# Two sequences per output projection, in three products of rounded parts, turned back by a transpose

## The chip, the cores and the metric

The kernel runs on one core of a Trainium2 chip. The metric is the device time of one execution in microseconds, lower is better. A profile of one execution comes with it: its span runs from the first to the last instruction, and all times inside it count from the start of the span.

## What is computed

A decoder layer over 16 sequences of 128 tokens with 128 features, all in float32. The part that matters here is the multi-head attention that is run twice, first on the layer's own tokens ("sa"), then against a context ("ca"), with 16 heads of 64 features:

```
def attention(x, ctx, mask, wq, wk, wv, wo, bo):
    q, k, v = (x @ wq), (ctx @ wk), (ctx @ wv)          # split into 16 heads of 64
    sim = jnp.einsum('bhid,bhjd->bhij', q, k) * SCALE
    sim = jnp.where(mask[:, None, None, :], neg, sim)
    attn = jax.nn.softmax(sim, axis=-1)
    out = jnp.einsum('bhij,bhjd->bhid', attn, v).transpose(0, 2, 1, 3).reshape(b, n, 1024)
    return out @ wo + bo                                # the output projection
...
a = attention(x, x, ...);   x = layernorm(x + a, ln1_g, ln1_b)
a = attention(x, ctx, ...); x = layernorm(x + a, ln2_g, ln2_b)
h = gelu(x @ fc1_w + fc1_b); x = layernorm(x + h @ fc2_w + fc2_b, ln3_g, ln3_b)
```

Ahead of it stands a convolution mixer with a layer norm, and behind it a small mixture of experts with a last layer norm.

## The kernel before, in words

All engines run orders written out by hand; every dependence is a semaphore wait in the code. The work of both attentions is one list of 32 items (`ITEMS`): item n is sequence n % 16 of attention n // 16. A loop over p from 0 to 31 (VectorE: 1 to 32) handles several stages of neighbouring items at once. I call one turn of it "loop p". In loop p TensorE does, in this order (lines 736 to 757):

- `x_transpose(p-4)`, the transpose of the item's normalised result into the layout that the next product needs;
- `v_half(p, 0)` and `(p, 1)`, the values, three products of 512 columns each;
- `unit(p, 0..3)`, queries and keys for a later pair of sequences, six products of 256 columns each. Units 0 and 2 write PSUM bank 0 and are copied out by ScalarE (`q_out`), units 1 and 3 write bank 1 and are copied out by VectorE (`k_out`);
- `transposes(p-1, 0..3)`, four probability tiles each, into banks 2 and 3 in turn, copied out by VectorE (`pt_out`, line 1107);
- in loops 0 to 9 products of the mixer (`projection`, `mixer_output`, `x1_transposes`);
- `out_proj(p-2)`, the output projection of one item: eight float32 products of 128 columns (line 582);
- `scores(p+1)` (line 551), into banks 0 to 3, and `p_v(p-1)` (line 566), into banks 4 and 5, copied out by ScalarE (`ot_out`, line 844).

The queries, keys and values are made in "three products of rounded parts" (`mm_split`, line 70): each operand is held as a rounded high part (type fp32r) and a low part (the rest, also fp32r), and high times high, high times low and low times high are summed in PSUM.

`scores(p+1)` must wait for both `k_out` of loop p, since it overwrites bank 1, and in its second half for all four `pt_out`, since it overwrites banks 2 and 3. VectorE then takes 16 tiles of scores with `maxima` (line 1081), ScalarE makes the exponentials (`exps`, line 817), VectorE the reciprocals of the sums, and GpSimd multiplies (`normalise(p, g)`, line 1530). After the output projection VectorE does `residual` (sum, statistics), GpSimd a power (`inverse_deviation`), VectorE `normalise`, GpSimd `affine` and `next_residual`, TensorE `x_transpose`, ScalarE `xT_high` and VectorE `xT_low`. The projection and `x_transpose` share bank 7 (`W_BANK`), so they wait for one another's readers.

After the loops comes a tail, also by hand: the hidden layer (`hidden`, `fc2_sum`, line 289) for four groups of four sequences, between the last projections, then the layer norms and the experts. Its order on VectorE opens with

```
residual(ITEMS - 1); xT_low(ITEMS - 2); normalise(ITEMS - 1); residual_sum(0)
residual_moments(0); xT_low(ITEMS - 1); gained(0); outer_sums(0)
```

where `residual_sum(g)` is line 1265 and `gained(g)` line 1279.

## Time and profile before

| | |
|---|---|
| median of 3 runs | 501.43 us (501.26 to 502.74) |
| the profiled execution's own time | 501.12 us |
| its span | 499.2 us |
| TensorE matmul busy | 470.6 us, 94% |
| VectorE busy | 385.0 us, 77% |
| ScalarE busy | 366.8 us, 73% |
| GpSimd busy | 251.9 us, 50% |
| mean granted TensorE clock | 0.99 of full speed |

The profiled execution took 1.9 us more than its span. PE stands for TensorE, DVE for VectorE, ACT for ScalarE, POOL for GpSimd. A share of the whole span is an average over stages that have different limits; busy times in a stretch say more. A matmul's duration holds a latency that overlaps the next matmul, so what a matmul costs is read from the distance of two starts.

### The profile page before, as it was taken

The numbers are of one execution on the slowest core, as the hardware profiler recorded it, in microseconds if no ns is written. First come the engines' busy times: TensorE is split into PE (matmuls) and PEld (weight loads), VectorE is DVE, ScalarE is ACT, GpSimd is POOL, SyncE is SP. The second block draws the span as 40 slices with busy tenths as digits, with TensorE's granted clock in tenths as the row PEclk, the third lists the DMA queues.
The fourth block names the chain that finished last, engine by engine and source line by source line (L and its number), as shares of the span: only waits on it lengthen the run. The fifth ranks groups of instructions, "written<-read, shape, count | busy, mean of one in ns | idle before, by whom it ended". The sixth has DMA issues, their size and how long they took to land.

```text
span 499.2 us, 14097 instructions
## 1 busy us (share of the span) xinstructions
PE 470.6 (94%) x4644; PEld 431.5 (86%) x4644; DVE 385.0 (77%) x1852; ACT 366.8 (73%) x1390; POOL 251.9 (50%) x342
## 2 busy tenths in 40 slices
PE   4788999999999999999999999999999999999894
PEld 4678889999999999999999999999999997798672
DVE  4768778898888877887787777777777777538866
ACT  3547887868677788877778887777777777836763
POOL 1545357675565654555545454444554455633432
PEclk9999999999999999999999999999999999999987
DMA  8740000000000004000000000000000000400003
GB/s 242 233 195 2 1 3 1 2 2 2 1 3 1 2 2 126 1 4 1 3 1 2 2 2 1 3 1 3 3 1 3 1 2 3 169 1 0 7 13 90
DMA packets 15720, 14.18 MB, mean 28 GB/s; under 512 B 2848, under 2 KB 13344, under 8 KB 15520
## 3 DMA queue, kind: packets, MB, share of 16 engines
q1 hardware_dynamic: 14080, 12.81, 8.2%
q8 instruction: 38, 0.62, 0.5%
q10 hardware_dynamic: 1568, 0.47, 0.5%
q14 instruction: 34, 0.28, 0.2%
HBM read 12.10 MB, written 1.18 MB: 27 GB/s over the span
## 4 chain that ended last, share of the span: by engine, by line
PE 73%; DVE 13%; ACT 5%; issue 3%; DMA 2%; POOL 2%; SPq 1%; POOLq 0%; DVEq 0%; ACTq 0%
PE late_bank L582 10%; PE late_bank L534 10%; PE late_bank L551 10%; PE late_bank L566 10%; PE late_bank L72 8%; PE late_bank L74 8%; PE late_bank L73 8%; ACT P L817 3%; DVE P L1081 3%; DMA x<-in_xT 2%; PE late_bank L591 1%; DVE G L1198 1%; DVE ffstats L1253 1%; PE late_bank L608 1%; PE late_bank L610 1%
## 5 line engine op out<-in xcount | busy, mean ns | idle before, releaser
L817 ACT ACTIVATE P<-P,at_negmax 128x128 f32<-128x128 f32 x512 | 198.9, 396 | 79.1 <-DVE at_negmax L1081 79.1
L1530 POOL TENSOR_TENSOR P<-P,at_inv 128x512 f32<-128x512 f32 x128 | 136.6, 1078 | 123.2 <-DVE at_inv L1091 123.1
L1107 DVE COPY at_PT<-late_bank 128x512 f32<-128x512 f32 x128 | 87.7, 688 | 35.1 <-PE late_bank L534 34.9
L1081 DVE CUSTOM_DVE_ANT_0 P<-late_bank,maskb 128x128 f32<-128x128 f32 x512 | 110.5, 286 | 2.7 <-PE late_bank L551 2.7
L817 ACT ACTIVATION_READ_ACCUMULATOR P<-P,at_negmax 128x1 f32 x512 | 100.1, 195 | 0.0
L534 PE MATMUL late_bank<-ident,P 128*128 128x128 f32 x512 | 76.4, 273 | 2.0 <-DVE at_negmax L1081 1.0
L534 PEld LDWEIGHTS late_bank<-ident,P 128*128 128x128 f32 x512 | 59.8, 140 | 8.5 <-issue 4.0
L551 PE MATMUL late_bank<-at_k,at_q 64*128 64x128 f32 x1024 | 65.8, 278 | 0.9 <-DVE at_k L1099 0.9
L551 PEld LDWEIGHTS late_bank<-at_k,at_q 64*128 64x128 f32 x1024 | 59.7, 188 | 4.8 <-issue 1.2
L566 PE MATMUL late_bank<-at_PT,V 128*64 128x128 f32 x1024 | 63.0, 276 | 0.0
L566 PEld LDWEIGHTS late_bank<-at_PT,V 128*64 128x64 f32 x1024 | 55.2, 137 | 3.9
L1099 DVE COPY at_k<-late_bank 128x512 f32<-128x512 f32 x64 | 44.2, 691 | 8.1 <-PE late_bank L74 7.0
L1081 DVE DVE_READ_ACCUMULATOR2_ANT at_negmax<- 128x1 f32 x512 | 42.7, 83 | 0.0
L827 ACT ACTIVATE at_q<-late_bank 128x512 f32<-128x512 f32 x64 | 37.7, 589 | 4.0 <-PE late_bank L74 4.0
L1548 POOL TENSOR_TENSOR at_N<-at_N,row_ln_g 128x128 f32<-128x128 f32 x32 | 14.7, 460 | 49.8 <-DVE at_N L1132 49.8
L836 ACT ACTIVATE V<-late_bank 128x512 f32<-128x512 f32 x64 | 37.6, 587 | 0.0
L844 ACT ACTIVATE at_OT<-late_bank 128x512 f32<-128x512 f32 x64 | 34.3, 587 | 2.9 <-PE late_bank L566 2.9
L608 PE MATMUL late_bank<-xT_hi,w_hi 128*128 128x256 f32 x72 | 22.8, 317 | 11.2 <-DVE xT_lo L1155 7.1
L582 PE MATMUL late_bank<-wo_sa,at_OT 128*128 128x128 f32 x256 | 31.3, 276 | 0.6 <-DVE x1T_lo L1234 0.6
L582 PE MATMUL late_bank<-wo_ca,at_OT 128*128 128x128 f32 x256 | 31.2, 275 | 0.0
L582 PEld LDWEIGHTS late_bank<-wo_sa,at_OT 128*128 128x128 f32 x256 | 29.9, 192 | 1.0 <-issue 1.0
L582 PEld LDWEIGHTS late_bank<-wo_ca,at_OT 128*128 128x128 f32 x256 | 29.9, 192 | 0.1
(195 smaller groups left out, 1055.4 us busy)
## 6 DMA issues: line engine op xcount, KB each, us to landing
ctxT_raw<-in_ctxT SPq DMA_DIRECT2D x1, 1024.0 KB, 8.8
out<-xres SPq DMA_DIRECT2D x4, 224.0 KB, 2.6
x<-in_xT SPq DMA_DIRECT2D x1, 768.0 KB, 9.5
xres<-in_x SPq DMA_DIRECT2D x1, 768.0 KB, 14.0
tap_rows<-in_short_wT SPq DMA_DIRECT2D x3, 192.0 KB, 4.9
sa_wq_raw<-in_sa_wq SPq DMA_DIRECT2D x1, 512.0 KB, 7.4
sa_wk_raw<-in_sa_wk SPq DMA_DIRECT2D x1, 512.0 KB, 8.5
sa_wv_raw<-in_sa_wv SPq DMA_DIRECT2D x1, 512.0 KB, 9.8
```

The costliest lines, as they stand in the source:

```text
L72: nc.tensor.matmul(out, w.hi[wsel], x.hi[xsel], start=first, stop=False)
L73: nc.tensor.matmul(out, w.hi[wsel], x.lo[xsel], start=False, stop=False)
L74: return nc.tensor.matmul(out, w.lo[wsel], x.hi[xsel], start=False, stop=True)
L534: last = nc.tensor.transpose(banks[T_BANK[g % 2]][:, h * 128:(h + 1) * 128], P[:, n % 2, HQ * g + h, :], k.ident[:])
L551: last = nc.tensor.matmul(score_bank(h), q[rows, t % 2, h // 2, pair], kk[rows, t % 2, h // 2, pair], start=True, stop=True)
L566: last = nc.tensor.matmul(banks[O_BANK[h // 8]][part:part + 64, h // 2 % 4 * 128:(h // 2 % 4 + 1) * 128], V[:, n % 2, h * DH:(h + 1) * DH] ...
L582: last = nc.tensor.matmul(banks[W_BANK][:, 0:128], OT[:, n % 2, c, :], out_w[att(n)][:, c, :], start=(c == 0), stop=(c == H // 2 - 1))
L817: last = nc.scalar.activation(P[:, n % 2, h, :], P[:, n % 2, h, :], ACT.Exp, scale=-1.0, bias=negmax[:, n % 2, h:h + 1], accum_out=total[: ...
L1081: last = nc.vector.tensor_tensor_reduce(P[:, n % 2, h, :], score_bank(h), k.maskb[:, cols(n)], scale=1.0, scalar=3.0e38, op0=ALU.add, op1= ...
L1099: nc.vector.tensor_copy(kk[:, t % 2, u - 1:u + 1, :], banks[UNIT_BANK[1]][:].rearrange("p (h l) -> p h l", h=2)).then_inc(k_ok, 1)
L1107: nc.vector.tensor_copy(PT[:, HQ * g:HQ * g + HQ, :], banks[T_BANK[g % 2]][:].rearrange("p (h l) -> p h l", h=HQ)).then_inc(pt_ok, 1)
L1530: nc.gpsimd.tensor_tensor(tile, tile, inv[:, n % 2, HQ * g:HQ * g + HQ].unsqueeze(2).to_broadcast([128, HQ, 128]), ALU.mult).then_inc(norm ...
```

## The change

The output projection takes a pair of items at once and is split. Its operands become high and low parts: `ot_out` (ScalarE) writes the high part, the new `ot_low` (VectorE) the low part, once per half item; ScalarE and GpSimd make the parts of the weights once for each attention. The product is made the other way round, with the weights stationary and the 256 columns of a pair moving, so it comes out transposed; ScalarE copies it out (`out_turned`) and two TensorE transposes turn it back (`turn_back`). Residual, statistics, normalisation, affine, `x_transpose`, `xT_high` and `xT_low` are done per pair. The projection is cut into two halves: the first stands ahead of `scores` in odd loops, the second behind `v_half(p, 0)` in even loops. Buffers that the parts need are found by overlaying others; so the context is loaded only after the mixer's last gate, and the second attention's output weights after loop 13. The low parts of the second attention's weights are made two loops later (loops 4, 6, 8 for 2, 4, 6).

```diff
+        FIRST_HALF, SECOND_HALF, NORM = -3, -4, -5
+        def item_pair(p, lag):
+            t = (p + lag) // 2
+            return t if (p + lag) % 2 == 0 and 0 <= t < PAIRS else None
...
+            sp.wait_ge(c_mm, 3 * NPAIR)
+            sp.wait_ge(y_ok, NPAIR)
             sp.dma_start(k.raw["ctxT"][:], io["ctxT"]).then_inc(ld_w["ctxT"], 16)
...
+            def out_proj(t, half):
+                pe.wait_ge(ot_lo, 4 * t + 3 + half)
+                if half == 0:
+                    wait(pe, xT_lo, t)
+                    wait(pe, r_ok, t)
+                    wait(pe, x1lo, before(t + 4))
+                    pe.wait_ge(wo_lo, att_pair(t) + 1)
+                w = out_w[att_pair(t)]
+                for c in range(4 * half, 4 * half + 4):
+                    for wo, ot in ((w.hi, OT.hi), (w.hi, OT.lo), (w.lo, OT.hi)):
+                        last = nc.tensor.matmul(banks[W_BANK][:, 0:PCOLS], wo[:, c, :], ot[:, c, :], ...)
+            def turn_back(t):
+                pe.wait_ge(outT_ok, t + 1)
+                for b in range(PAIR):
+                    last = nc.tensor.transpose(turned_back()[:, b], outT[:, b * 128:(b + 1) * 128], k.ident[:])
...
             for p in range(ITEMS):                                   # TensorE
-                x_transpose(p - 4)
                 v_half(p, 0)
+                out_proj(item_pair(p, SECOND_HALF), 1)
                 unit(p, 0)
                 transposes(p - 1, 0)
                 unit(p, 1)
+                turn_back(item_pair(p, SECOND_HALF))
                 v_half(p, 1)
                 transposes(p - 1, 1)
                 unit(p, 2)
                 x1_transposes(p, transposed_in(p))
+                x_transpose(item_pair(p, NORM))
...
-                out_proj(p - 2)
+                out_proj(item_pair(p, FIRST_HALF), 0)
                 scores(p + 1)
                 p_v(p - 1)
-            x_transpose(ITEMS - 4)
+            out_proj(PAIRS - 2, 1)
             transposes(ITEMS - 1, 0)
             transposes(ITEMS - 1, 1)
...
             hidden(k, pe, 0, (0, 1))
             second_bias(0)
+            turn_back(PAIRS - 2)
             transposes(ITEMS - 1, 2)
             transposes(ITEMS - 1, 3)
-            out_proj(ITEMS - 2)
             p_v(ITEMS - 1)
-            x_transpose(ITEMS - 3)
             hidden(k, pe, 0, (2, 3))
-            out_proj(ITEMS - 1)
             wait_result(1)
             hidden(k, pe, 1, (0, 1))
-            x_transpose(ITEMS - 2)
+            x_transpose(PAIRS - 2)
+            out_proj(PAIRS - 1, 0)
+            out_proj(PAIRS - 1, 1)
             fc2_sum(k, pe, 0)
-            x_transpose(ITEMS - 1)
+            turn_back(PAIRS - 1)
             hidden(k, pe, 1, (2, 3))
             wait_result(2)
             hidden(k, pe, 2, (0, 1))
             next_fc2(1)
+            x_transpose(PAIRS - 1)
             hidden(k, pe, 2, (2, 3))
...
-                xT_high(p - 4)                                       # ScalarE
                 v_out(p, 0)
+                ot_out(p - 2, 0)
+                out_turned(item_pair(p, SECOND_HALF))
                 q_out(p, 0)
+                ot_out(p - 2, 1)
                 mixer_normal(transposed_in(p))
-                ot_out(p - 2, 0)
-                ot_out(p - 2, 1)
                 exps(p, 2)
                 x1_high(transposed_in(p))
+                xT_high(item_pair(p, NORM))
...
+            def ot_low(n, o):                                        # VectorE
+                vec.wait_ge(ot_ok, 2 * n + o + 1)
+                part = np.s_[:, 4 * o:4 * o + 4, n % 2 * 128:(n % 2 + 1) * 128]
+                nc.vector.tensor_tensor(OT.lo[part], banks[O_BANK[o]][:].rearrange("p (c l) -> p c l", c=4),
+                                        f32(OT.hi[part]), ALU.subtract).then_inc(ot_lo, 1)
...
-                normalise(p - 3)
+                normalise(item_pair(p, NORM))
                 reciprocals(p, 0)
                 reciprocals(p, 1)
-                xT_low(p - 4)
                 pt_out(p - 1, 0)
+                ot_low(p - 2, 0)
                 k_out(p, 1)
+                ot_low(p - 2, 1)
+                residual(item_pair(p, SECOND_HALF))
                 pt_out(p - 1, 1)
+                statistics(item_pair(p, SECOND_HALF))
                 pt_out(p - 1, 2)
                 x1_low(transposed_in(p))
+                xT_low(item_pair(p, NORM))
                 k_out(p, 3)
                 pt_out(p - 1, 3)
...
-                if p in (2, 4, 6):
-                    weight_low(CA[p // 2 - 1])
+                if p in (4, 6, 8):
+                    weight_low(CA[p // 2 - 2])
...
-                residual(p - 2)
                 reciprocals(p, 3)
                 maxima(p + 1, 0)
                 maxima(p + 1, 1)
-            normalise(ITEMS - 2)
-            xT_low(ITEMS - 3)
-            residual(ITEMS - 1)
-            xT_low(ITEMS - 2)
-            normalise(ITEMS - 1)
+            ot_low(ITEMS - 1, 0)
+            ot_low(ITEMS - 1, 1)
+            normalise(PAIRS - 2)
+            xT_low(PAIRS - 2)
+            residual(PAIRS - 1)
+            statistics(PAIRS - 1)
             residual_sum(0)
+            normalise(PAIRS - 1)
             residual_moments(0)
-            xT_low(ITEMS - 1)
+            xT_low(PAIRS - 1)
             gained(0)
```

## Rows read from the trace of the kernel before

**Rows 1.** Windows: two loops of the mixer's stage, one later loop, the tail's two parts.
```profile
core 0: us, PE busy (x) PEld busy (x) DVE busy (x) ACT busy (x) POOL busy (x), PEclk, DMA share, GB/s
102.96:116.86 13.90, 13.82 (x143) 12.80 (x142) 11.49 (x57) 11.18 (x44) 8.95 (x11) 1.00 0.01 2
116.86:131.13 14.27, 14.27 (x149) 13.54 (x149) 12.23 (x57) 10.95 (x44) 8.35 (x12) 1.00 0.01 3
...
302.53:314.48 11.95, 11.95 (x129) 11.21 (x129) 9.41 (x48) 9.32 (x39) 5.96 (x9) 1.00 0.01 2
...
431.39:449.38 17.99, 17.99 (x169) 16.57 (x170) 7.07 (x24) 8.09 (x14) 7.43 (x16) 1.00 0.01 2
449.38:482.98 33.60, 30.78 (x192) 24.84 (x190) 28.21 (x142) 22.77 (x47) 13.19 (x13) 0.95 0.02 4
```

**Rows 2.** Timeline of TensorE through one later loop: start, us, what.
```profile
302.46 2.06 PE L551 MATMUL late_bank<-at_k,at_q 64*128 64x128 f32 x32
...
304.44 1.97 PE L566 MATMUL late_bank<-at_PT,V 128*64 128x128 f32 x32
...
306.34 0.33 PE L591 MATMUL late_bank<-ident,at_X 128*128 128x128 f32 x1
...
306.43 0.48 PE L72 MATMUL late_bank<-ca_wv_hi,ctxT_hi 128*128 128x512 f32 x1
...
307.21 0.28 PE L72 MATMUL late_bank<-x1T_hi,ca_wq_hi 128*128 128x256 f32 x1
...
307.93 0.60 PE L534 MATMUL late_bank<-ident,P 128*128 128x128 f32 x4
...
308.28 0.37 PE L72 MATMUL late_bank<-ctxT_hi,ca_wk_hi 128*128 128x256 f32 x1
...
309.08 0.40 PE L72 MATMUL late_bank<-ca_wv_hi,ctxT_hi 128*128 128x512 f32 x1
...
312.10 0.60 PE L534 MATMUL late_bank<-ident,P 128*128 128x128 f32 x4
...
312.53 1.95 PE L582 MATMUL late_bank<-wo_ca,at_OT 128*128 128x128 f32 x16
...
314.41 2.06 PE L551 MATMUL late_bank<-at_k,at_q 64*128 64x128 f32 x32
```

**Rows 3.** Timeline of VectorE in the same loop: the first maximum, and what follows the last.
```profile
303.67 0.29 DVE L1081 CUSTOM_DVE_ANT_0 P<-late_bank,maskb 128x128 f32<-128x128 f32 x1
...
307.05 0.34 DVE L1132 TENSOR_SCALAR at_N<-at_R,at_mv,at_rstd 128x128 f32<-128x128 f32 x1
```

**Rows 4.** Timeline of VectorE: two copies back to back; a mixer residual with its statistics.
```profile
434.66 1.28 DVE L1107 COPY at_PT<-late_bank 128x512 f32<-128x512 f32 x2
...
115.43 0.41 DVE L1207 TENSOR_TENSOR R<-late_bank,xres 128x256 f32<-128x256 f32 x1
...
116.76 0.17 DVE L1091 RECIPROCAL at_inv<-at_total 128x4 f32<-128x4 f32 x1
```

**Rows 5.** Groups by form: operations like those added or merged, mean ns of one.
```profile
L1265 DVE TENSOR_TENSOR ffR<-late_bank,xres 128x512 f32<-128x512 f32 x4 | 2.8, 690 | 2.2 <-PE late_bank L289 2.2
...
L844 ACT ACTIVATE at_OT<-late_bank 128x512 f32<-128x512 f32 x64 | 34.3, 587 | 2.9 <-PE late_bank L566 2.9
...
L1601 POOL TENSOR_TENSOR x<-N,row_ln_b 128x256 f32<-128x256 f32 x8 | 5.9, 733 | 0.0
```

**Rows 6.** Timeline of VectorE in loop 6: the last `pt_out`, then `weight_low` after the convolution.
```profile
128.49 0.68 DVE L1107 COPY at_PT<-late_bank 128x512 f32<-128x512 f32 x1
...
131.06 1.20 DVE L1239 TENSOR_TENSOR ca_wv_lo<-ca_wv_raw,ca_wv_hi 128x1024 fp32r<-128x1024 f32 x1
```

**Rows 7.** The tail: `fc2_sum(0)` in the chain of waits, VectorE's `residual_sum(0)` and `gained(0)`.
```profile
445.76 3.59 PE late_bank L289 x32
...
449.38 0.69 DVE L1265 TENSOR_TENSOR ffR<-late_bank,xres 128x512 f32<-128x512 f32 x1 [2.25 <-PE late_bank L289]
...
451.70 1.13 DVE L1279 SCALAR_TENSOR_TENSOR N<-ffR,ffmv,ln_g 128x128 f32<-128x128 f32 x4
```

**Rows 8.** DMA issues of the page: the load of the context, KB, us to landing.
```profile
ctxT_raw<-in_ctxT SPq DMA_DIRECT2D x1, 1024.0 KB, 8.8
```

More of the change, by code:

```diff
@@ L503, in unit @@
                     if a:
-                        wait(pe, xT_lo, 2 * t + 2 - NSEQ)
+                        wait(pe, xT_lo, t + 1 - NPAIR)
                     else:
@@ L584, in out_proj @@
                 last.then_inc(o_mm, 1)
-            def x_transpose(n):
-                if not exists(n):
+            def turn_back(t):
+                if t is None:
                     return
-                wait(pe, x_ok, n + 1)
-                wait(pe, r_ok, min(n + 2, ITEMS))
-                nc.tensor.transpose(banks[W_BANK][:, 0:128], X[:], k.ident[:]).then_inc(xT_mm, 1)
+                pe.wait_ge(outT_ok, t + 1)
+                for b in range(PAIR):
+                    last = nc.tensor.transpose(turned_back()[:, b], outT[:, b * 128:(b + 1) * 128], k.ident[:])
+                last.then_inc(back_mm, 1)
@@ L593, in projection, with x_transpose @@
+            def x_transpose(t):
+                if t is None:
+                    return
+                wait(pe, x_ok, t + 1)
+                wait(pe, x1lo, before(t + 5))
+                for b in range(PAIR):
+                    last = nc.tensor.transpose(banks[W_BANK][:, b * 128:(b + 1) * 128], X[:, b], k.ident[:])
+                last.then_inc(xT_mm, 1)
             def projection(p, m, c):
@@ L1127, in normalise @@
-            def normalise(n):
-                if not exists(n):
-                    return
-                vec.wait_ge(rstd_ok, n + 1)
-                wait(vec, x_ok, n)
-                nc.vector.tensor_scalar(N[:], R[:], mv[:, 0:1], rstd[:, 0:1], ALU.subtract, ALU.mult).then_inc(n_ok, 1)
-            def xT_low(n):
-                if not exists(n):
-                    return
-                vec.wait_ge(xT_hi, n + 1)
-                out = results[att(n)]
-                nc.vector.tensor_tensor(out.lo[:, cols(n)], banks[W_BANK][:, 0:128], f32(out.hi[:, cols(n)]),
+                vec.wait_ge(ot_ok, 2 * n + o + 1)
@@ new lines, in statistics @@
+            def statistics(t):
+                if t is None:
+                    return
+                vec.wait_ge(r_ok, t + 1)
+                for b in range(PAIR):
+                    last = nc.vector.bn_stats(stats[:, b], R[:, b])
+                last.then_inc(st_ok, 1)
+                vec.wait_ge(st_ok, 2 * t + 1)
+                for b in range(PAIR):
+                    last = nc.vector.bn_aggr(mv[:, b], stats[:, b])
+                last.then_inc(st_ok, 1)
+                vec.wait_ge(st_ok, 2 * t + 2)
+                nc.vector.tensor_scalar(mv[:, :, 1], mv[:, :, 1], EPS, None, ALU.add).then_inc(mv_ok, 1)
@@ new lines, in normalise, with xT_low @@
+            def normalise(t):
+                if t is None:
+                    return
+                vec.wait_ge(rstd_ok, t + 1)
+                wait(vec, x_ok, t)
+                for b in range(PAIR):
+                    last = nc.vector.tensor_scalar(N[:, b], R[:, b], mv[:, b, 0:1], rstd[:, b:b + 1], ALU.subtract,
+                                                   ALU.mult)
+                last.then_inc(n_ok, 1)
+            def xT_low(t):
+                if t is None:
+                    return
+                vec.wait_ge(xT_hi, t + 1)
+                out = results[att_pair(t)]
+                nc.vector.tensor_tensor(out.lo[:, pcols_pair(t)], banks[W_BANK][:, 0:PCOLS], f32(out.hi[:, pcols_pair(t)]),
```

225 lines of the change are left out of this document (128 added, 97 removed).

## The prediction

> **What bounds the kernel now.** I read three views in this order. The windows by loop [rows 1] show who is full: in the later loops TensorE is busy 11.95 of 11.95 us and VectorE 9.41, in the mixer's loops TensorE 13.82 of 13.90 and 14.27 of 14.27, VectorE 11.49 and 12.23. So TensorE sets the pace, and VectorE has 15 to 20% left. The tail is two stretches: up to 449.38 TensorE is again full (17.99 of 17.99); after it VectorE is (28.21 of 33.60, its waits being for GpSimd's powers in a chain with it). The timeline of TensorE [rows 2] then gives the place of each step in a loop, and that of VectorE [rows 3] how near it runs behind.
>
> I count from the start of `v_half(p, 0)` (306.43). Before it lie `scores` 1.98, `p_v` 1.90, `x_transpose` 0.09. Behind it: `v_half` 0.78, a unit 0.72 (0.80 behind transposes, as switching back from float32 costs 0.08), four transposes 0.35, their results 0.60 after their start; transposes(p-1, 0) at 1.50, `out_proj` at 6.10, next `scores` at 7.98 [rows 2].
>
> **The change on TensorE.** Removed in each loop: a projection, 1.88 from 312.53 to 314.41, and an `x_transpose`, 0.09 [rows 2]. Added for a pair: 24 products of 256 columns at 0.12 (six take the 0.72 of a unit), 2.86 in all or 1.43 a half; two turning transposes, 0.18 plus 0.08 for the switch; two `x_transpose` at 0.09 beside other transposes, 0.2. So `scores` comes at 7.98 - 1.88 + 1.43 + 0.26 = 7.79 in even loops, at 7.98 - 1.88 + 1.43 + 0.2 = 7.73 in odd ones, and a pair of loops needs 0.63 less TensorE time than the 23.9 it takes now. Over 16 pairs this is 10 us: all that the change can bring.
>
> **The change on VectorE.** Each `ot_low` reads 512 columns from PSUM and is priced by `residual_sum`, 690 ns [rows 5]; back to back such operations follow at 0.60 [rows 4] (unshown in this form; bounds are 0.60 and 0.69, I take 0.60). Two a loop add 1.2. Merging gives back some 0.2 a loop: one sum, one epsilon and one `xT_low` for two items. VectorE goes to about 10.4 of 11.6. That would fit on average; its order decides.
>
> *Even loop, later stage.* The second half of the projection now stands ahead of transposes(p-1, 0), so these start at 1.50 + 1.43 = 2.93 and end at 3.53. VectorE has ended the maxima and reciprocals by 1.6 and waits. From 3.55 to `scores` it must do, in order, `pt_out`, `ot_low`, `k_out`, `ot_low`, `residual`, `pt_out`, `statistics`, `pt_out`, `k_out`. Seven operations of 512 columns: 6 at 0.60 and the last at its full 0.69, 4.29. Residual and statistics of a pair take 1.33 in the mixer [rows 4], 1.2 here as a `pt_out` lies between. End: 9.05, and `scores` can start at 9.1 instead of 7.79, since it overwrites the bank that `k_out` reads: **1.3 us of waiting that is new**. Today three such operations stand there and nothing else. What is late next: `maxima(p+1)` start 1.21 after `scores` [rows 2, 3] and ScalarE follows them, so all shift by as much and nothing is made up. *Odd loop:* transposes end at 2.1, six operations end before 6.0, `xT_low` and `k_out` by 7.0, ahead of `scores`. But the first half waits for `xT_low` (same bank): `x_transpose` at 4.5 waits for GpSimd's two operations of 0.733 [rows 5], which start at 1.4, so it is in time; `xT_high` comes after `exps(p, 2)`, `xT_low` ends about 6.4 where 6.3 was wanted: 0.1. Sum for a later pair: -0.63 + 1.3 + 0.1 = +0.8.
>
> *Mixer's loops.* In even loops two projections stand between the transposes and `scores`, at 10.1, and the nine operations fit. But the convolution follows the last `pt_out`: that ends at 10.0, the convolution takes 1.97 (131.06 - 128.49 - 0.60), `weight_low` 1.20 [rows 6]. Maxima then start at 13.2 with `weight_low`, 1.9 late, end 3.38 later [rows 3], and the next loop's transposes, which overwrite score banks, wait 1.25 for them.
>
> *Other engines.* ScalarE gets a copy of 256 columns a pair and the weights' high parts; at 9.32 of 11.95 it stays hidden [rows 1]. GpSimd makes two low parts of weights in loops 2 and 17; with 5.96 to 8.95 busy per loop it hides them, and merged layer norms cost it nothing more. The context's load, 8.8 us [rows 8], moves behind loop 8's gate and is wanted at the end of loop 11, over 30 us later; if that cover went, ScalarE's rounding and the units of loop 15 would wait by as much as it is late. The second output weights load after loop 13 and are wanted in loop 19. All at nothing.
>
> **Stage by stage.** Loops 2 and 3: item 0's projection is gone from loop 2 (-1.9), loop 3 has a half instead of a whole (-0.45), and a `weight_low` went (-0.25): -2.6. Loops 4 to 7: two pairs at -0.63, two late `weight_low` at +1.0 beyond what is waited today: +0.7. Loops 8 to 11: loop 8 has convolution and `weight_low` with no projection to cover them: 1.4 ahead of `scores`, 1.9 more at the next transposes; loop 10 waits 1.4, of which some 0.9 are waited now; -1.3 of work: +2.5. Loops 12 to 29: nine pairs at 0.8, +7.2. Loops 30 and 31 have no units and follow the exponentials as now: 0.
>
> *The tail,* counted from the end of the last projection in a loop (431.39 now). Today: `fc2_sum(0)` ends at 18.0, `gained(0)` starts at 20.3 [rows 1, 7]. New on TensorE: `p_v` 1.9, the second half 1.5, transposes, two hidden chunks, bias, turn back at 6.3. VectorE waits for this with `residual` (6.5), and behind it stand `pt_out` 1, statistics, `pt_out` 2 and 3: end 9.65. `p_v` of the last item waits for that until 9.7 instead of 8.05, ends at 11.6. Its `ot_out` (0.59 each [rows 5]) and `ot_low` stand ahead of `normalise(14)`, 13.5; GpSimd's two operations: 15.15; `x_transpose(14)`, `xT_high`, `xT_low`: 16.45. Only then may the last pair's projection start in the same bank: 19.4, and `fc2_sum` (3.59) ends at 23.0, 5.0 later than now. Now VectorE: the last `residual` and statistics stand ahead of `residual_sum(0)`, and `xT_low(15)` ahead of `gained(0)`, while `x_transpose(15)` stands behind `fc2_sum(1)`: turn back 0.2, four hidden chunks 3.1, `fc2_sum(1)` 3.6, transpose, `xT_high` and `xT_low` 1.2: 31.1. **`gained(0)` starts 10.8 later than now**, and what follows is the chain VectorE bounds, so it shifts whole: +10.8.
>
> **Sum.** 501.12 (the profiled execution, 1.9 over its span, 0.3 under the median) - 2.6 + 0.7 + 2.5 + 7.2 + 10.8 = 519.7; I say 519.
>
> One rule speaks to the tail. The clock is at full speed in the full stretch before 449.38 and 0.95 of it after, where TensorE has gaps, so some time there ran at 1.2 GHz [rows 1]. In my schedule TensorE waits some 3.5 us for `residual_sum(1)` ahead of `fc2_sum(2)`; at 1.2 GHz that sum would take 3.6 more. The Trainium skill (TensorE: Matmul & The Clock Gate, "HAM oscillation") says that gaps between bursts re-throttle the array; the row agrees that the clock falls in this stage, and by the rule the time would be up to 523.
>
> **Rivals.**
> - *Loops stay TensorE's, the tail loses.* If VectorE's nine operations took 4.2 us instead of 5.5, no `scores` would wait; loops 4 to 31 would give about -9 and with -2.6 and the tail 500 to 506. For it: VectorE's average fits. Against it: 0.60 and 0.69 are rows, and nothing of the nine is optional.
> - *Faster.* The mechanism is the full 10 us of TensorE with the tail's work hidden. It needs the order on VectorE not to matter: `gained(0)` no more than about 8 us late with all loops bound by TensorE, 491 to 499. For it: the tail before 449.38 has VectorE busy only 7.07 of 17.99 [rows 1]. Against it: the queue is in order, and `xT_low(15)` waits behind `fc2_sum(1)` whatever VectorE's load.
> - *The clock falls in the tail, or even loops also hold back ScalarE*: 523 to 532. For it the clock's 0.95; against it, only one gap of mine is long.
> - *The change doesn't do what it says:* products are 24 a pair, by its own lines; not likely.
>
> **Numbers.** Forecast case 0.68 (510 to 524), TensorE-bound loops with a late tail 0.12, faster 0.08, slower still 0.12. The unknowns are `ot_low` (0.09 each, 60 times: 5 us), the fit of even loops (0.4 in eleven) and the tail's waits (half of 10.8). Cutting 5 off each side from these gives 507 to 529. A difference under 0.3%, 1.5 us, can't be told from none. Faster 0.10, same 0.04, slower 0.86.
>
> **What would show it.** Right: in even loops a wait of TensorE for `k_out` of 1 to 1.5 us ahead of `scores` and none in odd ones; loops of about 12.9 and 11.8; VectorE idle near 1.9 us before the first `pt_out` of even loops; `fc2_sum(0)` to `gained(0)` some 8 us apart for 2.3 now. Wrong: even loops below 12 us (VectorE's operations cheaper than priced), products of 256 columns further apart than 0.12, or the chain behind `gained(0)` having slack that takes up the delay.

## The result, and the profile after

The changed kernel takes 526.64 us (median of 4 runs, 524.42 to 527.35), the kernel before 501.35 (501.03 to 502.74) beside it: **1.049 times as long, 95% interval 1.046 to 1.052**. Forecast: 519, between 507 and 529. The profiled execution of after is its shortest, 524.42, span 522.5; that of before has a span of 499.2. The 23.3 between these two are what the views below place. Two executions (1116.51 us of the kernel before, beside e10 and e11, and 764.65 us of e12) were over half as long again as all others and are in no ratio.

The waits of TensorE in the profile after (line, what it waited for: us in total, times, longest us):

```profile
PE late_bank L588 <- DVE at_k L1171: 14.6, 12, 1.3
...
PE late_bank L298 <- DVE ffR L1357: 4.3, 2, 3.4
...
PE late_bank L603 <- DVE at_PT L1179: 1.4, 1, 1.4
```

The first line is new but for one of its waits: `scores` (L588) waits for `k_out` (L1171) in the eleven even loops from 8 to 28, 1.03 us in loops 8 and 10 and 1.3 us in each of the nine later ones, 13.7 in all. The twelfth, 0.88 us ahead of `scores(0)`, stands in the profile of before as well, and there it is the only one. The windows of after, by the same columns as [rows 1]: an even and an odd later loop, then the tail cut at the end of `fc2_sum(0)` and at the start of `gained(0)`:

```profile
297.40:310.49 13.09, 11.79 (x125) 10.98 (x125) 9.48 (x49) 9.87 (x41) 4.45 (x5) 1.00 0.01 2
310.49:322.44 11.95, 11.94 (x124) 11.00 (x124) 10.41 (x50) 9.51 (x39) 6.53 (x8) 1.00 0.01 2
...
444.10:467.40 23.30, 19.84 (x175) 17.24 (x175) 7.24 (x17) 8.56 (x14) 4.44 (x8) 1.00 0.01 2
467.40:475.38 7.98, 7.79 (x53) 6.79 (x52) 4.44 (x19) 3.19 (x6) 3.86 (x5) 1.00 0.00 1
475.38:508.00 32.62, 23.95 (x160) 19.18 (x158) 27.67 (x142) 22.06 (x47) 12.16 (x12) 1.00 0.03 5
```

The even loop is 1.3 longer than TensorE's busy time in it, and VectorE is busy for only 9.48 of its 13.09: the engine that TensorE waits for has room, but not at that place. The timeline of VectorE in this loop (start us, us) shows the queue that the prediction laid out against [rows 3]:

```profile
304.85 0.69 DVE L1179 COPY at_PT<-late_bank 128x512 f32<-128x512 f32 x1 [1.88 <-PE late_bank L571]
305.46 0.68 DVE L1188 TENSOR_TENSOR at_OT_lo<-late_bank,at_OT_hi 128x512 fp32r<-128x512 f32 x1
306.06 0.68 DVE L1171 COPY at_k<-late_bank 128x512 f32<-128x512 f32 x1
306.65 0.68 DVE L1188 TENSOR_TENSOR at_OT_lo<-late_bank,at_OT_hi 128x512 fp32r<-128x512 f32 x1
307.25 0.42 DVE L1200 TENSOR_TENSOR at_R<-late_bank,xres 128x256 f32<-128x256 f32 x1
307.58 0.68 DVE L1179 COPY at_PT<-late_bank 128x512 f32<-128x512 f32 x1
308.18 0.48 DVE L1207 BATCH_NORM_STATS2 at_stats<-at_R 128x6 f32<-128x128 f32 x2
308.69 0.25 DVE L1211 BATCH_NORM_AGGREGATE at_mv<-at_stats 128x2 f32<-128x6 f32 x2
308.98 0.17 DVE L1214 TENSOR_SCALAR at_mv<-at_mv 128x2 f32<-128x2 f32 x1
309.06 0.69 DVE L1179 COPY at_PT<-late_bank 128x512 f32<-128x512 f32 x1
309.66 0.68 DVE L1171 COPY at_k<-late_bank 128x512 f32<-128x512 f32 x1
```

It is idle for 1.88 until the first transposes (L571) come, behind the second half of the projection. From then on it never stops for 5.49 us (304.85 to 310.34); the last entry of these lines is the one that `scores` waits for. TensorE's own timeline closes the step:

```profile
301.28 0.50 PE L72 MATMUL late_bank<-ca_wv_hi,ctxT_hi 128*128 128x512 f32 x1
...
308.60 0.60 PE L571 MATMUL late_bank<-ident,P 128*128 128x128 f32 x4
310.49 0.71 PE L588 MATMUL late_bank<-at_k,at_q 64*128 64x128 f32 x8 [1.30 <-DVE at_k L1171]
```

`v_half` starts at 301.28, and the last transposes at 308.60 take 0.35 of issue, so `scores` could have started at 308.95, 7.67 behind `v_half`; it starts at 9.21. The 1.30 in brackets counts from the modelled end of the transposes, the full loss is 1.54.

The tail, on TensorE, answers to [rows 7]:

```profile
453.76 1.97 PE L603 MATMUL late_bank<-at_PT,V 128*64 128x128 f32 x32 [1.40 <-DVE at_PT L1179]
...
460.72 0.35 PE L621 MATMUL late_bank<-at_OT_hi,wo_ca_hi 128*128 128x256 f32 x1 [0.98 <-issue]
463.66 3.73 PE L298 MATMUL late_bank<-fc,P 128*128 128x128 f32 x32
...
470.64 3.73 PE L298 MATMUL late_bank<-fc,P 128*128 128x128 f32 x32
474.20 0.38 PE L641 MATMUL late_bank<-ident,at_X 128*128 128x128 f32 x2
...
481.16 3.84 PE L298 MATMUL late_bank<-fc,V 128*128 128x128 f32 x32 [3.38 <-DVE ffR L1357]
```

and on VectorE:

```profile
468.99 0.69 DVE L1357 TENSOR_TENSOR ffR<-late_bank,xres 128x512 f32<-128x512 f32 x1
...
475.04 0.42 DVE L1231 TENSOR_TENSOR x1T_lo<-late_bank,x1T_hi 128x256 fp32r<-128x256 f32 x1 [2.90 <-ACT x1T_hi L918]
475.38 1.13 DVE L1371 SCALAR_TENSOR_TENSOR N<-ffR,ffmv,ln_g 128x128 f32<-128x128 f32 x4
```

`gained(0)` (L1371) stands behind `xT_low(15)` (L1231), which waits 2.90 for a chain that begins with `x_transpose(15)` (L641) behind `fc2_sum(1)`: the averages that it reads had been ready since 471.7.

Where the 23.3 lie, by the starts of `scores` in both traces (it also has e7 and e10, told below):

| part | before, us | after | change | forecast | e7 | e10 |
|---|---|---|---|---|---|---|
| loops 2 and 3 | 28.83 | 26.73 | -2.1 | -2.6 | 26.73 | 26.70 |
| loops 4 to 7 | 56.34 | 57.83 | +1.5 | +0.7 | 56.51 | 56.50 |
| loops 8 to 11 | 49.93 | 52.71 | +2.8 | +2.5 | 50.39 | 50.38 |
| loops 12 to 29 | 215.16 | 225.52 | +10.4 | +7.2 | 219.96 | 214.66 |
| loop 30 to the end | 89.16 | 99.82 | +10.7 | +10.8 | 93.82 | 94.53 |
| an even / odd later loop | 11.95 / 11.95 | 13.09 / 11.96 | | 12.97 / 11.71 | 12.14 / 11.96 | 12.14 / 11.73 |

A loop here is counted from one `scores` to the next; up to loop 2 the two differ by 0.1.

### The profile page after: what moved, and what is told of

It is laid out like the page before. It is cut to its first block, busy times and chain, and to the rows that moved or that the text cites. A ratio compares the mean times of both kernels' runs of the same rounds, so it can differ in the third digit from the quotient of the medians.

```text
span 522.5 us, 13807 instructions
## 1 busy us (share of the span) xinstructions
PE 466.5 (89%) x4548; PEld 422.7 (81%) x4548; DVE 403.8 (77%) x1868; ACT 377.6 (72%) x1392; POOL 241.9 (46%) x280
## 4 chain that ended last, share of the span: by engine, by line
PE 57%; DVE 24%; issue 8%; ACT 3%; DMA 3%; POOL 2%; SPq 1%; POOLq 0%; DVEq 0%
PE late_bank L588 10%; PE late_bank L621 9%; PE late_bank L603 9%; PE late_bank L571 7%; PE late_bank L72 6%; PE late_bank L74 5%; PE late_bank L73 5%; DVE at_k L1171 4%; DVE P L1153 3%; DVE at_PT L1179 2%; DVE at_OT_lo L1188 2%; DMA x<-in_xT 2%; ACT P L871 2%; DVE G L1290 2%; PE late_bank L298 1%
## 5 line engine op out<-in xcount | busy, mean ns | idle before, releaser
L871 ACT ACTIVATION_READ_ACCUMULATOR P<-P,at_negmax 128x1 f32 x512 | 98.8, 193 | 0.0
L571 PE MATMUL late_bank<-ident,P 128*128 128x128 f32 x512 | 76.7, 273 | 5.5 <-DVE at_negmax L1153 3.5
L588 PE MATMUL late_bank<-at_k,at_q 64*128 64x128 f32 x1024 | 66.0, 278 | 15.0 <-DVE at_k L1171 14.6
L588 PEld LDWEIGHTS late_bank<-at_k,at_q 64*128 64x128 f32 x1024 | 60.1, 188 | 20.3 <-issue 17.4
L571 PEld LDWEIGHTS late_bank<-ident,P 128*128 128x128 f32 x512 | 59.8, 140 | 11.7 <-issue 6.6
L1640 POOL TENSOR_TENSOR at_rstd<-at_mv,half_neg 128x2 f32<-128x2 f32 x16 | 11.3, 706 | 82.7 <-DVE at_mv L1214 82.7
L1171 DVE COPY at_k<-late_bank 128x512 f32<-128x512 f32 x64 | 43.7, 683 | 6.4 <-PE late_bank L74 6.4
L881 ACT ACTIVATE at_q<-late_bank 128x512 f32<-128x512 f32 x64 | 37.9, 592 | 13.7 <-PE late_bank L74 13.7
L1188 DVE TENSOR_TENSOR at_OT_lo<-late_bank,at_OT_hi 128x512 fp32r<-128x512 f32 x64 | 43.5, 683 | 2.9 <-ACT at_OT_hi L898 2.6
L898 ACT ACTIVATE at_OT_hi<-late_bank 128x512 fp32r<-128x512 f32 x64 | 37.2, 584 | 3.6 <-PE late_bank L603 3.6
L1163 DVE RECIPROCAL at_inv<-at_total 128x4 f32<-128x4 f32 x128 | 20.5, 170 | 13.8 <-ACT P L871 12.5
L1651 POOL TENSOR_TENSOR at_N<-at_N,row_ln_g 128x256 f32<-128x256 f32 x16 | 11.8, 738 | 32.5 <-DVE at_N L1222 32.5
L659 PEld LDWEIGHTS late_bank<-xT_hi,w_hi 128*128 128x128 f32 x72 | 14.5, 201 | 12.3 <-issue 8.9
```

The lines of the kernel that those rows point to most:

```text
L571: last = nc.tensor.transpose(banks[T_BANK[g % 2]][:, h * 128:(h + 1) * 128], P[:, n % 2, HQ * g + h, :], k.ident[:])
L588: last = nc.tensor.matmul(score_bank(h), q[rows, t % 2, h // 2, pair], kk[rows, t % 2, h // 2, pair], start=True, stop=True)
L871: last = nc.scalar.activation(P[:, n % 2, h, :], P[:, n % 2, h, :], ACT.Exp, scale=-1.0, bias=negmax[:, n % 2, h:h + 1], accum_out=total[: ...
L881: nc.scalar.activation(q[:, t % 2, u:u + 2, :], banks[UNIT_BANK[0]][:].rearrange("p (h l) -> p h l", h=2), ACT.Copy, scale=NEG_SCALE).then ...
L1171: nc.vector.tensor_copy(kk[:, t % 2, u - 1:u + 1, :], banks[UNIT_BANK[1]][:].rearrange("p (h l) -> p h l", h=2)).then_inc(k_ok, 1)
L1188: nc.vector.tensor_tensor(OT.lo[part], banks[O_BANK[o]][:].rearrange("p (c l) -> p c l", c=4), f32(OT.hi[part]), ALU.subtract).then_inc(ot ...
```

## The experiments

**The theory** is that of the forecast case: two places in VectorE's order cost the time, the queue between the first transposes and `k_out(p, 3)` in even loops, and the last pair's place in the tail. **Rivals:** VectorE's added load as such (two `ot_low` a loop, 43.5 us in all), the place of the second half on TensorE, and the falling clock. Each of the kernels below is the changed kernel with one edit, from e7 on with several.

**e1: no low parts.** The calls of `ot_low` go, and the waits on them become waits on `ot_out`:

```diff
-                    for wo, ot in ((w.hi, OT.hi), (w.hi, OT.lo), (w.lo, OT.hi)):
+                    for j, wo in enumerate((w.hi, w.hi, w.lo)):   # all with OT.hi
...
-                ot_low(p - 2, 0)
-                ot_low(p - 2, 1)
```

> Leaves out the low part of the attention output: no ot_low on VectorE, and the second of the three products takes the high part again, so TensorE still makes all 24 products. If VectorE's queue between transposes(p-1, 0) and k_out(p, 3) is what holds scores in even loops, taking 1.2 us out of it takes 1.2 of the 1.3 us wait away: even loops go from 13.09 to about 11.9, the odd ones lose at most 0.2, the mixer's loops some, the tail about 1; median near 508 (from 526.6). If instead it is the turned product itself (its place ahead of the transposes, the shared bank 7, the turning back) that costs, the loops stay at 13.09 and 11.96 and the time within 2 us of 526.6.

Measured: 518.26 us, 1.034 times before (1.030 to 1.038). Even later loops take 12.44. Two operations of 0.60 went, but only 0.65 came back:

```profile
302.61 0.41 DVE L1200 TENSOR_TENSOR at_R<-late_bank,xres 128x256 f32<-128x256 f32 x1
303.36 0.69 DVE L1179 COPY at_PT<-late_bank 128x512 f32<-128x512 f32 x1 [0.33 <-PE late_bank L571]
```

The queue is now so early that its second `pt_out` waits 0.33 for the second transposes. So my 508 was wrong: I had taken the added time off the end of the queue and not looked at when each entry's input comes; the tail gained nothing either (91.5 us from the last `scores` to the end, after 89.6). As a verdict on load against order it says that without any load from the low parts TensorE still waits, 7.7 us in the eleven even loops.

**e2: statistics behind the last `pt_out`.** The same work in another place, in all loops:

```diff
-                statistics(item_pair(p, SECOND_HALF))
                 pt_out(p - 1, 2)
                 x1_low(transposed_in(p))
                 xT_low(item_pair(p, NORM))
                 k_out(p, 3)
                 pt_out(p - 1, 3)
+                statistics(item_pair(p, SECOND_HALF))
```

> The change, but statistics(t) stands behind pt_out(p-1, 3) on VectorE instead of ahead of pt_out(p-1, 2). Nothing waits for it before the next loop. By the queue theory the 0.88 us that it takes leaves the stretch ahead of k_out(p, 3): even loops from 13.09 to 12.2, wait for k_out from 1.3 to 0.4, eleven such loops: about -9 us, and 0.7 in the tail; median near 517. If VectorE's total work were the limit, moving an operation would change nothing: 526.

Measured: 523.22 us, 1.043 (1.036 to 1.050). Even later loops take 12.24, as the theory had it. But loops 5, 7 and 9 of the mixer went from 14.44, 14.40 and 13.93 to 15.33, 15.27 and 16.36, and loop 13 from 11.94 to 12.75: there the convolution or a low part stands behind the last `pt_out` and ahead of the next maxima, and the statistics came on top. The gain in one stage was paid back in the other, which I had not forecast.

**e3: another order in the tail.** On TensorE (VectorE and ScalarE follow, and VectorE takes `normalise(14)` ahead of the last `ot_low`):

```diff
+            turn_back(PAIRS - 2)
             hidden(k, pe, 0, (0, 1))
             second_bias(0)
-            turn_back(PAIRS - 2)
...
+            x_transpose(PAIRS - 2)
             wait_result(1)
             hidden(k, pe, 1, (0, 1))
-            x_transpose(PAIRS - 2)
             out_proj(PAIRS - 1, 0)
             out_proj(PAIRS - 1, 1)
-            fc2_sum(k, pe, 0)
-            turn_back(PAIRS - 1)
             hidden(k, pe, 1, (2, 3))
+            turn_back(PAIRS - 1)
+            fc2_sum(k, pe, 0)
+            x_transpose(PAIRS - 1)
             wait_result(2)
             hidden(k, pe, 2, (0, 1))
             next_fc2(1)
-            x_transpose(PAIRS - 1)
```

> The change with only the tail reordered: turn_back(14) ahead of the first hidden chunks, normalise(14) ahead of the last ot_low, x_transpose(14) one step earlier, hidden(1, (2, 3)) between the last pair's projection and its turn_back, that ahead of fc2_sum(0), and x_transpose(15) directly behind fc2_sum(0). By my schedule gained(0) starts about 6 us earlier (31.3 us after the last projection in a loop becomes about 25) and the chain behind it moves whole: median near 520. If the tail is bound by the amount of TensorE work, or the chain behind gained(0) has slack, less than 2 us come of it.

Measured: 519.01 us, 1.035 (1.031 to 1.040). The loops are those of after to 0.02; from the last `scores` to the end it is 81.8 us, where after has 89.6 and before 78.5. The timeline of VectorE shows why: no wait of 2.90 is left between the moments of group 0 and `gained(0)` (L1370), which now starts 24.9 behind the last projection in a loop, where after has 31.3.

```profile
467.41 0.69 DVE L1356 TENSOR_TENSOR ffR<-late_bank,xres 128x512 f32<-128x512 f32 x1 [0.71 <-PE late_bank L298]
...
469.54 0.42 DVE L1230 TENSOR_TENSOR x1T_lo<-late_bank,x1T_hi 128x256 fp32r<-128x256 f32 x1
469.87 1.13 DVE L1370 SCALAR_TENSOR_TENSOR N<-ffR,ffmv,ln_g 128x128 f32<-128x128 f32 x4
```

**e4: the last `k_out` by ScalarE**, in all loops but 0:

```diff
                 v_out(p, 1)                    # ScalarE
+                if p:
+                    k_out_late(p, 3)           # the same copy, by ScalarE
...
-                k_out(p, 3)                    # VectorE
                 pt_out(p - 1, 3)
```

> The change, but k_out(p, 3) of loops 1 to 29 is done by ScalarE behind v_out(p, 1), which takes 0.6 us off VectorE and puts 0.59 on ScalarE. By the queue theory k_out is then done about 8.15 us after v_half instead of 9.1: the wait ahead of scores goes from 1.3 to 0.4, even loops 12.2, about -10 us; median near 517. If ScalarE has no room (exps of the next loop late), the gain is under 3 us and ACT's wait for maxima, 68.5 us in all now, shrinks without gain.

Measured: 519.88 us, 1.036 (1.031 to 1.041). Even loops take 12.14, odd ones still 11.96; loops 13, 17 and 19 have 12.28, 12.87 and 12.86, of which more below, and loop 2 went from 13.19 to 14.19, which I had not forecast. VectorE's queue was what `scores` waited for; the 0.36 us that is left in each even loop is a wait for the same copy on ScalarE.

**e5: the second half behind the first transposes:**

```diff
-                out_proj(item_pair(p, SECOND_HALF), 1)
                 unit(p, 0)
                 transposes(p - 1, 0)
+                out_proj(item_pair(p, SECOND_HALF), 1)
```

> The second half of the projection stands behind unit(p, 0) and transposes(p-1, 0) instead of ahead of them; nothing is left out or reordered on VectorE. Theory (VectorE's queue between the first transposes and k_out(p, 3) is what TensorE waits for): VectorE gets its first pt_out 1.43 us earlier, but the two ot_low and the k_out of unit(p, 1) behind it then start earlier too, and residual still has to wait for the turned result, which comes no earlier than now; so only a part of the 1.43 comes through: even loops 12.7 for 13.09, 522 to 523 us in all. Rival (it is only the place of the half): the whole wait of 1.3 goes in each of the later even loops and 1 us in the mixer's even loops, 509 to 511 us.

Measured: 521.64 us, 1.040 (1.037 to 1.043); even loops 12.69, in the mixer 14.10 for 14.50. VectorE's timeline: its first `pt_out` is no longer late by 1.88, but the queue stops at its third entry.

```profile
300.71 0.69 DVE L1179 COPY at_PT<-late_bank 128x512 f32<-128x512 f32 x1 [0.43 <-PE late_bank L571]
301.32 0.68 DVE L1188 TENSOR_TENSOR at_OT_lo<-late_bank,at_OT_hi 128x512 fp32r<-128x512 f32 x1
302.88 0.69 DVE L1171 COPY at_k<-late_bank 128x512 f32<-128x512 f32 x1 [0.87 <-PE late_bank L74]
```

So the place of the half on TensorE is not the cause by itself: 0.40 a loop comes back, not 1.3, as said beforehand.

**e7: several places at once.** All the work is kept: the tail of e3; `k_out(p, 3)` by ScalarE in even loops from 4 on; the statistics behind the last `pt_out` from loop 12 on only; and

```diff
-                if p in (4, 6, 8):
+                if p in (5, 7, 9):
                     weight_low(CA[p // 2 - 2])
```

> All of the work is kept, its order is not: the tail's order of e3, k_out(p, 3) of the even loops from 4 on by ScalarE, the statistics behind the last pt_out from loop 12 on only, and weight_low in loops 5, 7 and 9 instead of 4, 6 and 8. Theory (a few queue places cost the time, and their costs add up): even later loops 12.1 for 13.09, odd ones 11.96, so loops 12 to 29 give back 8.5 us; the tail gives back 7.5; loops 4 to 11 give back about 2.5 (even loops lose the late weight_low, about 1 us each in three loops, odd loops get up to 0.3 each). 526.6 - 18.5 = about 507 us (505 to 510). Rival (the three gains cover one another, since all of them give VectorE's time): 513 us or more.

Measured: 509.34 us, 1.015 (1.012 to 1.018). The table has it by parts: loops 4 to 11 lose 3.6 of the 4.3 that they had cost. Loops 5, 7 and 9 give 0.67, 0.67 and 1.17 of this; the copy of k on ScalarE alone gave 0.16, 0.14 and 0.04 there (e4), so some 0.5, 0.5 and 1.1 are the place of `weight_low`. The other 1.1 is the copy's, in loops 8 and 10. The gains add up, except in loops 13, 17 and 19: 12.70, 12.88 and 13.45.

**e8 and e9.** e8 is e7 with one edit more, which gives TensorE something to do while ScalarE copies (the copy of these values goes behind `exps(p, 3)` on ScalarE). e9 is e8 with `xT_low` ahead of `pt_out(p-1, 2)` from loop 12 on and another order in the tail: `fc2_sum(0)` stands ahead of the last pair's projection, and that pair's `residual` and statistics stand behind `gained(0)` on VectorE.

```diff
                 transposes(p - 1, 3)
+                if p % 2 == 0 and p >= 12:
+                    v_half(p, 1)               # was ahead of transposes(p-1, 1)
```

> e7, and in even loops from 12 on v_half(p, 1) stands behind transposes(p-1, 3) and its copy behind exps(p, 3), so that TensorE has work while ScalarE makes k_out(p, 3). Theory: the last 0.34 us of TensorE's wait for k_out goes in each of nine even loops, even loops 11.8, 503 to 504 us. Rival (ScalarE's exponentials or VectorE's maxima set the pace below 12.1): even loops stay at 12.1, 507 us.

> e8, and from loop 12 on xT_low stands ahead of pt_out(p-1, 2), and in the tail fc2_sum(0) stands ahead of the projection of the last pair, whose residual and statistics come behind gained(0) and outer_sums(0) on VectorE, with GpSimd's two powers for group 0 ahead of those for the last pair. Theory: odd loops 11.80 for 11.96 (TensorE no longer waits 0.17 for xT_low ahead of the first half), 1.4 us in nine loops; gained(0) some 5 us earlier than in e8, of which 3 come through because the last pair's x_transpose and hidden(3) come later. 503.5 - 1.4 - 3 = 499 us (497 to 502), so no slower than the kernel before. Rival (the tail's end is set by the last pair's result and not by group 0): 502 us, the same as the kernel before.

Measured: e8 510.89 us, 1.017 (1.014 to 1.021), even loops 12.23 for 12.14. Nothing was gained, as the rival had it, but not for the rival's reason. From loop 12 on the wait for `k_out` is gone, and another of nearly its size stands ahead of the last transposes (L571), whose bank VectorE's second `pt_out` has to empty first:

```profile
304.92 0.63 PE L571 MATMUL late_bank<-ident,P 128*128 128x128 f32 x4 [0.32 <-issue]
```

VectorE ended that `pt_out` at about 304.8 (started as the first of two at 304.14). e9: 507.64 us, 1.015 (1.011 to 1.019). Its odd loops take 11.72, for 11.96: the 0.24 that TensorE had lost there came from `xT_low`'s place in VectorE's queue. The tail did not gain the 3 us forecast: from the last `scores` to the end the profiled executions have 86.7 us for e9 and 84.5 for e8, both at a mean clock of 0.982.

**e10: e9 with the large single operations moved too** (ScalarE's high part of the context also comes earlier), and e8's edit taken back:

```diff
-                elif p in (12, 13):
-                    context_low(p - 12)
-                elif p == NSEQ:
+                elif p in (11, 13):
+                    context_low(p // 2 - 5)
+                elif p == NSEQ + 1:
                     feed_forward_low()
-                elif p == NSEQ + 2:
+                elif p == NSEQ + 3:
                     bias_low()
```

> e9 with v_half(p, 1) back in its old place, and with the low parts of the context, of the feed-forward weights and of the biases made on VectorE in loops 11, 13, 17 and 19 instead of 12, 13, 16 and 18 (ScalarE's high part of the context one loop earlier where the load allows it). Theory (e8 only moved TensorE's wait from k_out(p, 3) to VectorE's pt_out ahead of the last transposes; and loops 13, 17 and 19 of e7 to e9 are late because a large extra operation on VectorE stood in the even loop ahead of them, which in the changed kernel the wait for k_out covered): even later loops 12.14 for 12.23, loops 13, 17 and 19 within 0.4 of the 11.72 of the other odd ones, 2 to 3 us less than e9: 504 to 506 us. Rival (VectorE is simply full, so the work comes up in another loop): 507.5 us, and loops 12 to 20 add up to as much as in e9.

Measured: 504.60 us (median of 12 runs), 1.0056 (1.0032 to 1.0081). Loops 13, 17 and 19 take 11.69, 11.73 and 11.73. VectorE was not full; these operations had stood in even loops, behind the last `pt_out` and ahead of the next maxima. In the changed kernel the 1.3 us for which `scores` waits in the same even loop had covered them: the first maximum of loops 13, 17 and 19 starts 1.65, 1.20 and 1.82 us behind its `scores` there, 2.47, 2.64 and 3.22 in e7, and 1.54 in e10. In loops 17 and 19 of e7 part of this is a wait of the low part for ScalarE's high part (0.60 and 0.99). This is the best of my versions, and it is still 0.6% slower than the kernel before.

**e11: products that fill two waits of the tail**, nothing else:

```diff
+            filler(13)                         # 128x512 products, result unread
             next_fc2(2)
...
+            filler(12)
             z_transposes(1)
```

> The changed kernel with 25 more products of 128x512 in the tail, whose result nobody reads (their bank is written anew later): 13 where TensorE waits 3.4 us ahead of fc2_sum(2) and 12 where it waits 3.2 us ahead of z_transposes(1), 3.05 and 2.8 us of work, so that they fit in the waits. Theory (the clock falls behind these waits in most executions, though not in the one profiled; that is why the median stands 2.2 us over the profiled execution): the mean clock is 0.99 or more in nearly all runs, and the median 524 to 525 us, below 526.6. Rival (the clock does not go by these waits, or its falls cost nothing): clocks from 0.98 on as before and 526 to 527 us, or more by the products' own time.

Measured: 526.19 us (522.84 to 526.97, 6 runs), 1.048 (1.045 to 1.051). The waits shrank from 3.38 to 0.38 and from 3.23 to 0.44, and the mean clocks are 0.989 to 0.997 where the four runs of after have 0.979 to 0.995. The median fell by 0.45, which is less than these runs scatter. My theory that the median would come down to 524 to 525 is not borne out. In e11's profiled execution the granted clock is 1.00 from 420 to 450 us, 0.83 in the window from 450 to 460, and 1.00 again up to 508: that fall comes ahead of both filled waits, so filling them could not prevent it.

**e12: e10 with the tail of e3, and ScalarE copies k ahead of v:**

```diff
-                v_out(p, 1)
                 if p % 2 == 0 and p > 2:
                     k_out_late(p, 3)
+                v_out(p, 1)                    # from loop 12 on, in even loops
```

> e10 with the tail of e3, and in even loops from 12 on ScalarE copies k_out(p, 3) ahead of v_out(p, 1) instead of behind it. Theory: the copy starts with the end of unit(p, 3) and not 0.2 us behind it, so TensorE's last wait of 0.36 shrinks to 0.15 to 0.2 and even loops take 11.95 to 12.0 for 12.14, 1.3 to 1.7 us in nine loops; the tail costs 3 us over that of the kernel before. 504.6 - 1.5, and the tail's end within 1 us of e10's: 502 to 503.5 us, 0.1 to 0.5% over the kernel before. Rival (v_out a little later holds back exps(p, 3) and with it the next transposes): even loops shorter and odd ones longer by as much, 504 to 505 us.

Measured: 506.03 us, 1.011 (1.007 to 1.015). Even loops stay at 12.14, odd ones go from 11.73 to 12.06: no gain, and the price that the rival had named in odd loops (0.33 each) with it. From the last `scores` to the end it has 82.2 us, e10 84.3 in its profiled execution, whose clock was 0.985 against 0.994.

## Why the prediction was right, step by step

**The mechanism was right**, and by the view that was to show it. `scores` waits 1.30 for `k_out` in even later loops (said: 1.3; between 1 and 1.5) and in none of the odd ones; VectorE stands idle 1.88 ahead of the first `pt_out` (said: near 1.9); its queue takes 5.49 (said: 5.5); `ot_low` follows at 0.60 like a copy. e2 and e4 take one entry out of this queue, by its place and by its engine, and give back 0.85 and 0.95 a loop. In the tail the last item's `p_v` starts 9.66 behind the last projection in a loop (said: 9.7), the last pair's projection 16.62 (said: 16.45), `fc2_sum(0)` ends 23.3 behind it (said: 23.0), and 8.0 pass from there to `gained(0)` (said: 8).

**The size was partly off.** The median of 526.64 lies above the forecast case's own 510 to 524 and 7.6 above the 519; it is inside the range of 507 to 529, and by its number alone it would fall to the case of 523 to 532. What the traces show is the mechanism of the forecast case with terms that were too small. The range does not quite follow from its own working either: its three unknowns (5, 4.4 and 5.4 us) add up to 14.8, and with 5 off that is 9.8 on each side of 519, 509 to 529.

**TensorE's saving was right in the later loops**, 0.63 a pair, though by two misses that cancel. Even loops: ready for `scores` at 7.67 (said: 7.79), with `scores` and `p_v` 11.55. Odd loops: 11.73 in e10, where nothing stands in their way (said: 7.73, with the same two 11.61). Together 23.28, the forecast's own sum, but the even loop is 0.12 shorter than said and the odd one 0.12 longer: that is luck. The 11.55 was never reached, though; 12.14 is what the best runs have (e10: `scores` starts 0.59 late, behind ScalarE's copy). e8 shows what stands behind one wait there, namely the next one in VectorE's queue.

**Mis-sized terms.**
- *Loops 12 to 29, +7.2 forecast, +10.4 measured.* A pair costs 1.14 and not 0.8, by three parts. The first is the step "`xT_low` ends about 6.4 where 6.3 was wanted: 0.1". VectorE took `xT_low` only behind the `pt_out` ahead of it, at 320.33; TensorE was ready for the first half at 320.59 (transposes 320.24, 0.35 of issue) and started it at 320.85. That is 0.26 (e9: 0.24), for I had placed `xT_low` by its input and not by its queue:

```profile
320.33 0.41 DVE L1231 TENSOR_TENSOR x1T_lo<-late_bank,x1T_hi 128x256 fp32r<-128x256 f32 x1
...
320.85 0.36 PE L621 MATMUL late_bank<-at_OT_hi,wo_ca_hi 128*128 128x256 f32 x1
```

  The second part, 0.12, is TensorE's work in odd loops, in which the switch from these products back to `scores` costs 0.08 (322.24 to 322.44, for a spacing of 0.12). The third, 0.11, stands in even loops: `scores` starts at 9.21, not 9.1, 0.15 behind the end of the copy.
- *Loops 4 to 7, +0.7 forecast, +1.5 measured.* The late `weight_low` was put at 1.0 a pair and is some 0.5 by e7 and e4. What failed is the other part, "-0.63" of TensorE's work a pair, with no wait beside it: with `weight_low` and the copy of k out of the way (e7) a pair takes 28.27 (14.50 and 13.77) against 28.18 before. In the even loops the wait that holds them is one that the forecast did not have. `x1_transposes` (L685) writes the same bank 7 in which the turned result lies until VectorE's `residual` (L1200) has read it:

```profile
125.96 0.41 PE L685 MATMUL late_bank<-ident,N 128*128 128x128 f32 x2 [0.24 <-DVE at_R L1200]
```

  The product ahead of it starts at 125.45 and takes 0.12 of issue, so 0.39 is lost (in loop 6 of e7 it is 0.26 ahead of `turn_back` and 0.08 here). In e5 and e1 `residual` is in time, this spacing is 0.12, and these loops take 14.10 and 14.07. In the odd loops of e7 the first transposes start 0.51 and 0.48 later than the products ahead of them would let them, waiting for the maxima; before, that was 0.24. These two come to 0.65 of the 0.72 that are missing.
- *Loops 8 to 11, +2.5 forecast, +2.8 measured.* This near hit is partly luck too. Loops 8 and 9 cost 2.1 where the forecast's terms give 1.4 + 1.9 - 0.63 = 2.7, and loops 10 and 11 cost 0.7 where they give 0.5 - 0.63 = -0.1. The wait of 0.39 for `residual` stands in loops 8 and 10 as well.
- *Loops 2 and 3, -2.6 forecast, -2.1 measured.* Loop 2 gave its 1.93; loop 3 gave 0.17 and not 0.7.
- *The tail, +10.8 forecast:* +11.0 up to `gained(0)`, 0.4 back behind it and 0.1 in loops 30 and 31.

**The sum** of the misses, 0.5 + 0.8 + 0.3 + 3.2 - 0.1 = 4.7, takes 519.7 to the 524.42 of the profiled execution. The median is 2.2 above that.

**The clock.** In the profiled execution the granted clock stayed at 1.00, the higher level, through the wait of 3.38 us and up to 508 us. In e5's trace, with the same tail and the same wait (474.7 to 478.12), it fell to 0.50, the lower level, while TensorE stood idle in it:

```profile
472.09:475.49 3.40, 2.46 (x10) 1.42 (x8) 3.33 (x13) 1.37 (x2) 0.00 (x0) 1.00 0.00 0
475.49:478.89 3.40, 0.77 (x3) 0.77 (x4) 2.25 (x13) 1.39 (x4) 1.99 (x2) 0.68 0.00 0
478.89:482.29 3.40, 3.40 (x18) 3.40 (x17) 3.12 (x17) 2.94 (x7) 1.11 (x1) 0.50 0.02 5
```

These are three windows by the columns of [rows 1]; TensorE was busy for 0.77 of the second, and 1.00 and 0.50 are its levels of 2.4 and 1.2 GHz. So the same schedule has its clock fall in one execution and not in another. The Trainium skill (TensorE: Matmul & The Clock Gate, "HAM oscillation") tells of a kernel in which the gap between two bursts re-throttled the array each time; e5's trace agrees, after's does not. What one fall costs can be read from the sum behind this wait, `fc2_sum(2)`:

```profile
478.12 6.40 PE L298 MATMUL late_bank<-fc,V 128*128 128x128 f32 x32 [3.38 <-DVE ffR L1357]
484.36 0.60 PE L699 MATMUL late_bank<-ident,N 128*128 128x128 f32 x4
```

From its start to the next transposes are 6.24 us in e5 and 3.67 in after (481.16 to 484.83), 2.57 more. The forecast had 3.6 more for this sum, all of it at the lower level; the clock was back at 1.00 before the end of it. From the last `scores` to the end e5 has 91.6 us and after 89.6, and e5's clock also fell once before that wait (0.77 from 450 to 456 us). The 2.2 us between the profiled execution and the median would fit such falls, but no trace of after's slower runs is kept. Among e10's twelve runs the time goes with the clock (502.57 us at 0.994, 505.82 and 507.91 at 0.982), but e11 raised the lowest clock from 0.979 to 0.989 and the median hardly moved, so what the falls cost over the whole kernel stays open.

**The rival "faster"** needed VectorE's order not to matter. The order could be mended in the loops: e10 runs from `scores(0)` to `scores(31)` in 384.15 us, before in 386.59. That is 2.4 of the 10 us that TensorE has less to do. 4.0 stay in eleven waits for ScalarE's k by the list of waits, which counts from modelled ends; by the starts each later even loop loses 0.59. The tail is 3.3 (e3) to 5.8 us (e10) longer than before. I take that to come from the last pair's projection, which starts only when both of its items are done, but no run here separates the two items in the tail.

## What to carry to other kernels

An engine that is idle for over a quarter of a loop (VectorE here, busy for 9.48 of 13.09 us) can still be what all wait for: lay out its queue between the event that starts it and the entry that is waited for, entry by entry, with the time at which each input comes. Shortening such a queue gives back only as much as its next late input allows (e1: 0.65 of 1.2), and a wait that goes uncovers what it had hidden (loops 13, 17 and 19). Where two items are merged into one step, look at the last pair at the end of the program first: the end cost 10.7 us here, and all loops together 12.6. And where two results share a bank, each wait for its reader is a term of the sum (0.39 a loop here).

## What was not expected of the hardware

- TensorE's clock does not follow from the schedule alone: beside e10 the mean clock of the kernel before lay between 0.982 and 0.997, that of e10 between 0.982 and 0.995, and the times go with it (before: 503.60 us at 0.982, 500.04 at 0.996). Differences under 1% need many runs of both kernels for this reason alone.
- Switching from products of rounded parts back to float32 products costs 0.08 beyond the spacing of 0.12, as switching out of transposes does (after: 322.24 to 322.44).
- Back-to-back operations of 128x512 on VectorE that read PSUM start 0.60 apart and last 0.68 each, for a copy and for a subtraction with a second operand from SBUF alike (304.85, 305.46, 306.06, 306.65).
